# A state space layer on one core: other slots for logarithms, remainders, a copy of sums and the scaling

## The reference, cut to what matters

```python
xz = xt @ in_proj
xc, z = (xz[..., :D_INNER], xz[..., D_INNER:])
xp = jnp.pad(xc, ((0, 0), (D_CONV - 1, 0), (0, 0)))
xconv = conv_b
for kk in range(D_CONV):
    xconv = xconv + conv_w[:, kk] * xp[:, kk:kk + T, :]
xc = jax.nn.silu(xconv)
dbc = xc @ x_proj
dt = jax.nn.softplus(dbc[..., :DT_RANK] @ dt_w + dt_b)
...
dA = jnp.exp(dt[..., None] * A)
dBx = (dt * xc)[..., None] * Bm[:, :, None, :]
def step(hprev, inp):
    dA_t, dBx_t, C_t = inp
    hnew = dA_t * hprev + dBx_t
    y_t = jnp.einsum('bds,bs->bd', hnew, C_t)
    return (hnew, y_t)
...
y = jnp.swapaxes(ys, 0, 1) + Dp * xc
y = y * jax.nn.silu(z)
return y @ out_w + out_b
```

## Time and profile before

| | us |
|---|---|
| median of 3 runs | 3880.18 |
| lowest and highest | 3868.65, 3884.69 |
| profiled execution | 3872.9 |
| its span | 3871.1 |
| state space layer: first and last start of a scan | 510.5, 2112.4 |
| busy in the span: PE, PEld | 3157.2, 2179.9 |
| busy in the span: DVE, ACT, POOL | 2993.0, 2599.1, 2375.2 |

### The profile page before, as it was taken

The page is one execution under the profiler, slowest core; times in us unless marked ns, Lnnn a source line. Parts: engine busy times, 40 slices in busy tenths (PEclk is TensorE's granted clock), DMA queues, the critical chain, the costliest instruction groups (busy, mean ns, idle before and its releaser), DMA issues. The chain is left out here.

```text
span 3871.1 us, 82456 instructions
## 1 busy us (share of the span) xinstructions
PE 3157.2 (82%) x29152; PEld 2179.9 (56%) x29152; DVE 2993.0 (77%) x5896; ACT 2599.1 (67%) x5235; POOL 2375.2 (61%) x2879
## 2 busy tenths in 40 slices
PE   7999579999999999999987777688848866578486
PEld 3776346666666666666665454366636533357355
DVE  3999569999999999999998466389958763178754
ACT  4888389999999999999995210166756463077562
POOL 2899478898998988888884000168755230044850
PEclk7999689999999999999999567777768877789698
DMA  3000100000000000000000512500000013500424
GB/s 93 24 24 26 48 7 13 24 24 23 24 22 20 19 23 24 24 23 24 23 18 21 141 46 93 201 29 23 12 6 1 1 25 122 208 5 1 117 59 125
DMA packets 271006, 172.53 MB, mean 45 GB/s; under 512 B 41648, under 2 KB 249976, under 8 KB 268536
## 3 DMA queue, kind: packets, MB, share of 16 engines
q1 hardware_dynamic: 270600, 167.25, 15.1%
HBM read 116.59 MB, written 50.60 MB: 43 GB/s over the span
## 5 line engine op out<-in xcount | busy, mean ns | idle before, releaser
L1223 DVE TENSOR_TENSOR_SCAN mam_hs<-mam_dA,mam_ps_b 128x1024 f32<-128x1024 f32 x512 | 1141.6, 2271 | 83.7 <-issue 43.8
L1143 ACT ACTIVATE mam_dA<-mam_dt,mam_A 128x496 f32<-128x496 f32 x1024 | 658.7, 710 | 0.4
L1005 PE MATMUL mam_ps_h<-mam_ident,mam_hs 128*128 128x128 f32 x4096 | 548.9, 277 | 64.0 <-ACT mam_hTb L1151 36.0
L1005 PEld LDWEIGHTS mam_ps_h<-mam_ident,mam_hs 128*128 128x128 f32 x4096 | 453.3, 142 | 229.2 <-issue 150.7
L1151 ACT COPY mam_hTb<-mam_ps_h 128x512 f32<-128x512 f32 x768 | 423.7, 588 | 95.9 <-PE mam_ps_h L1005 95.9
L991 PE MATMUL mam_ps_b<-mam_DB,mam_dtxt 32*128 32x512 f32 x2048 | 292.1, 637 | 78.1 <-DVE mam_hs L1223 74.0
L1017 PEld LDWEIGHTS mam_ps_y<-mam_hTb,mam_WC 128*32 128x32 f32 x8192 | 209.0, 110 | 133.1 <-issue 124.3
L1017 PE MATMUL mam_ps_y<-mam_hTb,mam_WC 128*32 128x128 f32 x8192 | 276.7, 276 | 0.3 <-issue 0.3
L774 POOL TENSOR_TENSOR mam_cv<-mam_cv,mam_tap 128x512 f32<-128x512 f32 x180 | 238.9, 1327 | 14.1
L810 POOL TENSOR_TENSOR mam_WC<-mam_cp,mam_m 128x128 f32<-128x128 f32 x512 | 194.3, 410 | 19.9 <-POOL mam_cv L774 14.8
L1233 DVE COPY mam_hTb<-mam_ps_h 128x512 f32<-128x512 f32 x256 | 174.3, 681 | 37.3 <-PE mam_ps_h L1005 35.4
(11 more groups left out here) (721 smaller groups left out, 8280.3 us busy)
## 6 DMA issues: line engine op xcount, KB each, us to landing
moe_wg<-in_L_ffn_weight SPq DMA_DIRECT2D x32, 1024.0 KB, 8.2
rnn_xr<-x SPq DMA_DIRECT2D x23, 512.0 KB, 6.3
l1y_wh<-mode_weights SPq DMA_DIRECT2D x16, 544.0 KB, 3.8
gat_hg<-in_x SPq DMA_DIRECT2D x16, 512.0 KB, 7.2
h<-gat_out SPq DMA_DIRECT2D x32, 256.0 KB, 2.3
mam_ht<-h SPq DMA_DIRECT2D x128, 64.0 KB, 2.0
mam_hr<-h SPq DMA_DIRECT2D x128, 64.0 KB, 2.0
mam_xt<-in_x SPq DMA_DIRECT2D x128, 64.0 KB, 2.1
```

Of the source, the lines that this page charges most:

```text
L1005: last = pe.transpose(ps_h[n][:, q * P:(q + 1) * P], hs[:, w % 3, c:c + P], ident[:, :])
L1143: act.activation(dA[:, h, :, n, 1:], dt[:, i % 2, h, :].rearrange("p (q t) -> p q t", q=Q)[:, :, 1:], ACT.Exp, scale=A[:, h, n:n + 1]).the ...
L1223: dve.tensor_tensor_scan(hs[:, w % 3, :], dA[:, h, first:first + 2, :, :].rearrange("p q s t -> p (q s t)"), ps_b[:, 2 * (w % 2):2 * (w % ...
```

## The change

Seven things move, and the arithmetic of each stays:

1. ACT: `logarithms(k+1)` goes from slot 8, behind the Silus, to slot 5, behind the states' copy there and ahead of the gates' Silus; the first `silu_z` goes from the head of slot 5 to slot 6, the second from 7 to 8, and `tokens_in` stands between the two `silu_x`.
2. ACT: the 16 `decays` of half 0 of the next turn are spread over slots 8 to 14 instead of 9 to 15.
3. POOL: `time_steps(k+1, 0)` and `(k+1, 1)` go from slot 9 to slot 7, around `spread_c` and `bias`; `plus(k+2, 0)` goes from slot 15 to the head of slot 14.
4. PE: the second `gate` goes from slot 6 to 7, `turn_tokens` from the end of slot 7 to the head of slot 8.
5. DVE: `lost` goes from slots 5 and 7 to slot 15 of the turn before (half 0) and slot 3 (half 1).
6. The copy of the sums of half 0 goes from ACT (slot 10) to DVE (slot 11); half 1 stays on ACT.
7. DVE: `statistics` goes from slot 11 to 13, where `moments` is; `scale` goes from slot 15 to slot 5 of the next turn, and `residual` gets a wait for it.

```diff
@@ -849,27 +849,27 @@
                     if turn(k + 2) and k + 2 >= EARLY:
                         convolve(k + 2, 1)
                 if u == 7:
+                    if turn(k + 1):
+                        time_steps(k + 1, 0)
                     if turn(k):
                         spread_c(k, 3)
                     if turn(k - 1):
                         bias(k - 1)
+                    if turn(k + 1):
+                        time_steps(k + 1, 1)
                 if u in (9, 11, 13, 15) and turn(k + 1):
                     spread_b(k + 1, (u - 9) // 2)
-                if u == 9 and turn(k + 1):
-                    time_steps(k + 1, 0)
-                    time_steps(k + 1, 1)
                 if u == 11 and turn(k - 2):
                     finish(k - 2)
                 if u == 14:
+                    if turn(k + 2):
+                        plus(k + 2, 0)
                     if turn(k + 1):
                         spread_c(k + 1, 0)
                     if turn(k - 1):
                         deviations(k - 1)
-                if u == 15:
-                    if turn(k + 2):
-                        plus(k + 2, 0)
-                    if turn(k + 1):
-                        spread_c(k + 1, 1)
+                if u == 15 and turn(k + 1):
+                    spread_c(k + 1, 1)
 
         @block.tensor
         def _(pe):
@@ -1021,6 +1021,8 @@
 
             for w in SLOTS:
                 k, u = divmod(w, U)
+                if u == 8 and turn(k + 3):
+                    turn_tokens(k + 3)
                 if u == 12 and turn(k + 1):
                     split_c(k + 1)
                 if u == 14 and turn(k + 1):
@@ -1035,10 +1037,8 @@
                     project_x(k + 2, u // 2)
                 if u in (1, 3) and turn(k - 1):
                     turn_sums(k - 1, u // 2)
-                if u in (4, 6) and turn(k + 2):
-                    gate(k + 2, (u - 4) // 2)
-                if u == 7 and turn(k + 3):
-                    turn_tokens(k + 3)
+                if u in (4, 7) and turn(k + 2):
+                    gate(k + 2, (u - 4) // 3)
                 if u == 8 and turn(k - 1):
                     project_out(k - 1)
                 if u == 10 and turn(k + 2):
@@ -1151,30 +1151,26 @@
                 act.copy(hTb[:, gg % 2, j, :, :], ps_h[n][:, :].rearrange("p (q d) -> p q d", q=S4)
                          ).then_inc(hB_ready if n else hA_ready, 1)
 
-            def sums_in(i, h):
-                act.wait_ge(y_done, i * 8 + 4 * h + 4)
-                act.wait_ge(yT_done, 2 * i + h)
+            def sums_in(i):
+                act.wait_ge(y_done, i * V + V)
+                act.wait_ge(yT_done, 2 * i + 1)
                 act.copy(ytok[:, :], ps_y[:, :]).then_inc(y_read, 1)
 
-            first1, first0 = (0, 3, 6, 9, 12, 16), (0, 2, 4, 7, 9, 11, 14, 16)
+            first1, first0 = (0, 3, 6, 9, 12, 16), (0, 2, 5, 7, 10, 12, 14, 16, 16)
             for w in SLOTS:
                 k, u = divmod(w, U)
                 if u == 0 and turn(k):
                     turned_steps_in(k, 1)
                 if u == 2 and turn(k - 1):
-                    sums_in(k - 1, 1)
-                if u == 10 and turn(k):
-                    sums_in(k, 0)
-                if u in (5, 7) and turn(k + 2):
-                    silu_z(k + 2, (u - 5) // 2)
+                    sums_in(k - 1)
                 if u == 8:
+                    if turn(k + 2):
+                        silu_z(k + 2, 1)
+                        silu_x(k + 2, 0)
                     if turn(k + 3):
                         tokens_in(k + 3)
                     if turn(k + 2):
-                        silu_x(k + 2, 0)
                         silu_x(k + 2, 1)
-                if u == 8 and turn(k + 1):
-                    logarithms(k + 1)
                 if u == 11 and turn(k + 2):
                     states_of_input(k + 2)
                 if u == 12 and turn(k + 1):
@@ -1187,12 +1183,16 @@
                     states_in(w - 1, 0)
                     if u % 2 == 0:
                         states_in(w - 1, 1)
+                if u == 5 and turn(k + 1):
+                    logarithms(k + 1)
+                if u == 6 and turn(k + 2):
+                    silu_z(k + 2, 0)
                 if u in (0, 2) and turn(k + 2):
                     x_in(k + 2, u // 2)
                 if u < 5 and turn(k):
                     decays(k, 1, first1[u], first1[u + 1] - first1[u])
-                if 9 <= u and turn(k + 1):
-                    decays(k + 1, 0, first0[u - 9], first0[u - 8] - first0[u - 9])
+                if 8 <= u and turn(k + 1):
+                    decays(k + 1, 0, first0[u - 8], first0[u - 7] - first0[u - 8])
 
         @block.vector
         def _(dve):
@@ -1247,9 +1247,15 @@
                 STT(out=y[:, h, :], in0=xs[:, i % 3, h, :], scalar=dp[:, h:h + 1], in1=ps_0[:, :],
                     op0=ALU.mult, op1=ALU.add).then_inc(y_taken, 1)
 
+            def sums_in(i):
+                dve.wait_ge(y_done, i * V + G)
+                dve.wait_ge(yT_done, 2 * i)
+                dve.tensor_copy(ytok[:, :], ps_y[:, :]).then_inc(y_read, 1)
+
             def residual(i):
                 dve.wait_ge(outed, i + 1)
                 dve.wait_ge(hr_ready, i + 1)
+                dve.wait_ge(scaled, i)
                 TT(z[:, :, :], hr[:, i % 2, :, :], ps_0[:, :].rearrange("p (g c) -> p g c", g=G), ALU.add
                    ).then_inc(z_ready, 1)
 
@@ -1286,16 +1292,19 @@
                     convolve(k + 2, u // 2 - 1)
                 if u == 3 and turn(k - 1):
                     take_y(k - 1, 1)
-                if u in (5, 7) and turn(k + 1):
-                    lost(k + 1, (u - 5) // 2)
+                if u == 3 and turn(k + 1):
+                    lost(k + 1, 1)
+                if u == 5 and turn(k - 2):
+                    scale(k - 2)
                 if u == 9 and turn(k - 1):
                     residual(k - 1)
-                if u == 11 and turn(k - 1):
+                if u == 11 and turn(k):
+                    sums_in(k)
+                if u == 13 and turn(k - 1):
                     statistics(k - 1)
-                if u == 13 and turn(k - 1):
                     moments(k - 1)
-                if u == 15 and turn(k - 1):
-                    scale(k - 1)
+                if u == 15 and turn(k + 2):
+                    lost(k + 2, 0)
 
 
 
```

## The result

| | before | after |
|---|---|---|
| median us | 3878.2 (4 runs) | 4018.7 (4 runs) |
| lowest and highest | 3868.7, 3884.7 | 4004.0, 4026.5 |
| profiled execution, its span | 3872.9, 3871.1 | 4026.5, 4024.7 |
| first and last start of a scan | 510.5, 2112.4 | 511.3, 2260.6 |

The changed kernel is slower by 1.036 (95% interval 1.0336 to 1.0383). The forecast was 3959 us, its range 3888 to 4000: the direction held, the size did not. The layer's scans now span 1749.3 us instead of 1601.9. Of the 154 us between the two profiled executions 147 lie there, nearly all in the 28 full turns: these take 55.58 on the mean instead of 50.40, which is 5.2 more for each, where the walk had 2.9.

What follows compares the result with a forecast made beforehand. No engine had much free, so the order within a turn was taken to bound it. Eight pairs summed to 53.3 us against 50.39, +2.9 over 28 turns, giving 3959 us; own range 3921 to 4007, over all cases 3888 to 4000.

Steps and rivals of the forecast that it cites:

- P7: Last scan pair, slots 14 and 15: 1.49 stall goes, scale leaves, lost comes; from 8.45 to 6.0 us (5.8 to 6.7).
- P0: First scan pair of a turn, slots 0 and 1: side work as before, stays 5.80 us.
- P1: Scan pair of slots 2 and 3: lost of half 1 added; from 5.81 to 7.1 us (6.5 to 7.5).
- P4: Scan pair of slots 8 and 9: turn_tokens moves in and PE's lead goes; from 5.80 to 6.7 us.
- P5: Scan pair of slots 10 and 11: sums copy comes to DVE, statistics leaves; from 6.01 to 5.80 us.
- P6: Scan pair of slots 12 and 13: statistics joins moments, 0.25 added for POOL; from 5.85 to 7.2 us.
- P2: Scan pair of slots 4 and 5: scale, held by POOL's convolution, takes 3.9 (3.6 to 4.9); from 6.03 to 8.9 us.
- P3: Scan pair of slots 6 and 7: no side work, ACT caught up, PE's floor; from 6.64 to 5.80 us.
- Rival 1: Whole turn: stall goes and all additions fit; 49.5 us a turn, 3855 us; chance 0.13.
- Rival 2: Slot 5: scale not held, P2 6.1 and P3 6.4, rest as walked; 3889 us; chance 0.11.
- Rival 3: Slot 5: first starter gets the port, so scale's rest slips through, P2 6.5; 3902 us; chance 0.10.
- Rival 4: End of turn: stall of P7 stays and the rest is added; over 4000 us; chance 0.04.

Runs made afterwards that it cites:

- decays14: Kernel before with only the 16 decays of half 0 issued in slots 9 to 14 instead of 9 to 15; 3884.3 us, 1.0006.
- noconv1: Changed kernel with POOL's second convolution left out from turn 3 on (stale values); 3888.3 us, a single run.
- scale15: Changed kernel with only scale put back into slot 15; 3937.5 us, 1.0159 against the kernel before.
- b_scale5: Kernel before with only scale moved to slot 5 of the next turn; 3991.8 us, 1.0315.
- warm: Changed kernel with PE's input matmuls of pair 3 issued four times, writing the same values; 4005.0 us, 1.0336 against the kernel before.
- silu_first: scale15 with the first gate's Silu ahead of the logarithms in slot 5, one table load more; 3981.7 us, 1.0263 against the kernel before.
- dve_part: Kernel before with DVE's moves alone, including the copy of sums but not scale's move; 3884.6 us, 1.0018.
- stat11: scale15 with statistics back in slot 11; 3944.5 us, 1.016 against the kernel before.

## Why the prediction came out as it did

**The stall of P7** goes, as forecast: the scan that starts a turn (1056.20) has no idle time before it, and P7 is 5.80 where 6.0 was said. decays14 shows that the decays' end is what the stall hung on. It also shows what the forecast of this term left out and got away with: removed by itself, the stall comes back in P4.

**P0, P1, P4, P5, P6** came within 0.25: 5.91, 7.23, 6.45, 5.80, 7.21. The lost lead of PE in P4, called a weak term, was right in kind: its copy waits 0.79 for PE's flip and starts 5.25 after the pair. The 0.25 added for the 128x4 instruction in P6 was right too (0.45 against 0.17).

**P2, a term mis-sized.** The mechanism was right, and noconv1 settles it: without POOL's operations the four take 1.10. The size was 3.9 and is 4.89 from start to start (1018.95 to 1023.84; 4.97 with the end of the last). The mis-sized term is the 0.3 for the first of the four. It assumed that DVE arrives near the end of an operation of POOL. It arrives as one starts and is held for all of it, in 27 of the 28 turns. The upper bound, 4.9, was the value. P2: +0.95. One reading behind it was turned round: the operation of POOL of 1.60 beside `lost` is some 0.33 longer than its kind (1.27), so there it is POOL that was held. Holding goes both ways; beside `scale` in slot 5 it went DVE's way only.

**P3, the step that failed.** The step was "no side work, so PE's floor, 5.80 ... behind the long P2 ACT has caught up". About ACT it is right: the gate in P3 does not wait for it. But the long P2 leaves PE nothing to do for 4.41 us, and PE comes back at 0.55 to 0.60 of its clock. The forecast walked through PE's durations at full clock because every row of before had them, and asked of the long pair only who gets time to catch up, not what the idle engine does afterwards. That is 1.3 in most turns and 2.3 in 8 of the 28, 1.54 on the mean. scale15 (1.00 in every turn) and noconv1 (1.00 in 27 of 28) without the long P2, and b_scale5 (0.51 behind it), tie the regular fall to the held `scale`; warm shows P3 at 5.80 where the clock stays up. silu_first shows that it is PE's pause that counts and not `scale` as such.

**The sum.** A turn came out 55.35 or 56.62 where 53.3 was said: 0.95 from P2, 1.3 or 2.3 from P3, the rest of the pairs cancel to within 0.3. Over 28 turns with a mean of +5.2 that is 145 of the 147 us; the forecast had 79. The bounds of the forecast were added up unevenly: its lower ones give its 51.9, but its upper ones (P1 7.5, P2 9.86, P6 7.55, P7 6.7, the rest as forecast) give 55.7 a turn and some 4027 us, not 55.0 and 4007. That the result lies under 4027 is luck: P1, P6 and P7 stayed below their bounds, and P3, which had none, went over.

**The parts by the runs.** From 3878 the order on DVE without the scaling costs some 7 us (dve_part, 1.0018), the parts on ACT, PE and POOL some 55 more (scale15 against dve_part, 1.0159 - 1.0018), the scaling's move 81. This holds in this order of adding; the parts are not independent, since the scaling's move alone costs b_scale5 3.15%.

**The rivals.** Rival 1 needed `scale` to be short at slot 5, and it is not. Rival 2's walk was good under its condition, as noconv1 shows. Rival 3's outcome (the rest of `scale` slips through a gap, 1.5 in all) did not come: each of the three was held for a whole operation. Its rule, who starts first gets the port, has the recorded starts against it, by 0.07 or 0.08. Rival 4 did not happen; the time above 4000 came from P2's size and the clock together, some 27 and 43 us. No rival had the clock, and the range, made of bounds from full-clock rows, ended below the result for that reason: with P2 right and P3 at its floor the sum is some 3986.

**Open.** What decides in which turns the clock falls: warm and silu_first show the same wait of PE just ahead of both outcomes, and noconv1 falls in one turn of 28. That ACT's, PE's and POOL's parts cost 1.9 a turn is measured as a whole; that the logarithms' new place on ACT has most of it is argued from PE's gate waiting 1.27 for `mam_sz`, and silu_first shows only that the other order is worse.

## What to carry to other kernels

Before moving a run of short SBUF-to-SBUF instructions on VectorE, look at what GpSimd does at the new place: beside its back-to-back operations each cost one of them here, the first included. When a pair becomes long by such a hold, ask of each engine that is left idle not only whether it catches up, but at what clock it comes back, and keep a bound for that in the range. And take a stall away together with the step that it gave time to: with the decays earlier, nothing was gained (1.0006) until the Silu that waited for GpSimd had been put behind the copies that PE waits for, and then little (0.9965).

## What of the hardware was not expected

- A VectorE instruction that the trace shows starting 0.07 us ahead of GpSimd's was held for all of it, 1.44, 1.21 and 1.42 us, where in noconv1 all four together took 1.10. By the recorded starts alone, then, one can't tell which of the two is held. Even one of 128x4 went from 0.17 to 0.45, and to 1.23 in stat11.
- TensorE came back near 1.2 GHz after pauses of 4.41 (clock 0.55, then 0.60), 2.77 (0.51) and 2.21 us (0.50), but in another turn with the pause of 2.21 it kept full speed. In warm it was at 0.66, on the mean of 5 us, behind a pause of 1.18 us, which in the next turn left it at 1.00.
